# One core, an adaLN transformer block: two thirds of the modulation moved into the first token tile, a bias row behind head 0, a row of maxima in front of the last values

## The chip, the cores and the metric

The kernel runs on one core of one Trainium2 chip. The metric is the device time of one execution in microseconds, as the median of several runs. Its engines are named TensorE (PE, with its weight loads PEld), VectorE (DVE), ScalarE (ACT), GpSimd (POOL) and SyncE (SP), each with its own instruction queue; SP, ACT and POOL also issue DMAs.

## The reference

Input x is 2 x 2048 x 512 in float32. From c (2 x 512) come six vectors for each of the two batches:

```python
mod = (_silu(L0_c) @ L0_wmod).reshape(L0_c.shape[0], 6, 1, -1)
sa, ca, ga, sb, cb, gb = (mod[:, 0], mod[:, 1], mod[:, 2], mod[:, 3], mod[:, 4], mod[:, 5])
ga = (2 * (ga >= 0) - 1) * jnp.maximum(jnp.abs(ga), 0.25)
gb = (2 * (gb >= 0) - 1) * jnp.maximum(jnp.abs(gb), 0.25)
h = _layernorm(x, axis=-1) * (1 + ca) + sa
x = x + ga * attention(h)        # 16 heads of 32, softmax, output projection and bias
h = _layernorm(x, axis=-1) * (1 + cb) + sb
x = x + gb * ffn(h)              # silu(h W1) * (h W3), Hadamard transform of 2048, W2
```

`attention` and `ffn` stand here for the reference's own functions. The first layer norm needs the shift sa and the scale ca alone. The gate ga is first used at the output projection, and sb, cb and gb later still.

## The kernel before

Products that need more than one pass's precision are made from high and low halves: each operand is rounded to fp32r (the high half, written by ScalarE), the difference is the low half (written by VectorE), and three matmuls (high by high, high by low, low by high) are summed. The program is a row of blocks; at the end of each, all engines meet before the next begins.

**Preparation** (`prepare`, lines 57 to 286). SyncE loads the identity, the attention weights in four groups, the first token tile, the modulation's weights `wm` (four chunks of 128 rows by 6 x 512), the output weights `natp`, the Hadamard matrix and the second token tile, through one queue in the order of lines 134 to 146. TensorE transposes the weights (`turn_rows`, L159), ScalarE and VectorE split them. TensorE then transposes the first token tile (`turn_tokens`, L294), makes the modulation's products (`modulate`, L179: per chunk four products of 32 columns into one PSUM bank, SA, CA, SB and CB, each in its own column group, and two, GA and GB, into another bank, in the first two column groups), transposes the output weights (`turn_out`, L172) between them, and at last the modulation (`turn_mod`, L189). ScalarE copies the products out (L236, L237) and writes shifts and scales (L244, L246). VectorE turns the raw gates into gains by four instructions, each waiting for the one before (L281 to L286).

**Projection of queries, keys and values** (`project_qkv`, L369). Eight tiles of 512 tokens. Each tile has NJ = 12 results of 12 matmuls (L538): 8 of queries and keys, 4 of values, in turn in BANKS = 4 PSUM banks. For each tile ScalarE applies shift and scale to the transposed tokens chunk by chunk (`high_parts`, L581), VectorE does the same in full precision for all four chunks (L625) and then makes the four low parts (L630). TensorE waits for all of them (L526, L527) before the tile's first result. ScalarE reads each result (L595, L599) and VectorE makes its low half (L637). Before the results of tile t, ScalarE normalises tile t + 1 (L304) from statistics that VectorE measures (L327 to L339). After result 5 the next tile is transposed. GpSimd makes butterflies of the Hadamard transform on W2 (L704). In the last 15 results TensorE also makes products for head 0's and 1's score maxima (L518), which VectorE reduces (L655); the row of maxima of head 0 is split by L648 and L650. SyncE stores the results in tile order: for each tile the queries and keys (L444) and, after the tile's last result, the values (L446, L447). In front of the first tile it waits for the gains and stores them (L457 to L459). After the last tile's values it sends the two rows of maxima (`send_max_row`, L365), which the first score of head 0 needs (L1027).

**Attention** (`attend`, L780). 32 heads. TensorE goes through 8 pairs of key tiles per head; each has 8 products for the maxima of a later head (L987), alternating with 8 scores (L1036), and then a burst that weighs values (L1047). There are 4 banks for maxima, reduced by VectorE (L1211), and 3 for scores, read by ScalarE's exponential (L1158). GpSimd adds up the exponentials (L1288, L1318), partly by DMAs (L1301); its first sum waits for every stored result (L1339), because its sums lie over their buffers. SyncE first loads the values of heads 0 and 1, queries, keys and values of head 2, the output bias (L963) and the gains. ScalarE's first instruction waits for that bias and copies its high half (L1195, L1196), VectorE's second makes the low half (L1257, L1258). Both are used behind attention only, at L1583.

**Output projection and feed-forward** (`project_and_feed`) follow. Nothing of them is changed.

## Time and profile before

| | us |
|---|---|
| median of 3 runs | 3136.89 |
| lowest and highest run | 3132.02, 3137.76 |
| the profiled execution's own time | 3138.33 |
| its span | 3136.5 |
| TensorE matmuls busy | 3077.2 (98% of the span) |
| VectorE, ScalarE, GpSimd busy | 1878.3, 1516.8, 1418.8 |

The profile covers one execution. In it, times count from the span's start. A group's idle time is that of its engine just before it, with what ended it. TensorE's clock is given as the share of full speed that was granted in a stretch. Matmuls overlap, so one's duration is longer than the step from one to the next. A float32 product of the modulation, whose operands are not split, is two records. The projection's tiles run from about 43 to 375 us, attention from about 379 to 1935, the rest to the end.

### The profile page before, as it was taken

The page shows a single profiled execution, that of the slowest core. Times are in us where ns is not written, and L with a number is a line of the kernel's source. Part 1 is how long each engine was busy: PE and PEld are TensorE (multiplying, and loading weights), DVE is VectorE, ACT ScalarE, POOL GpSimd, SP SyncE. Part 2 cuts the span into 40 slices and gives each one's busy share as a digit, 9 for nine tenths or more (in the row PEclk, how much of TensorE's full clock was granted, in tenths as well). Part 3 has the DMA queues.
Part 4 walks back from the last instruction along what each step waited for, and adds up shares of the span by engine and source line. Part 5 has one row for each costly group of instructions (what it writes and reads, how often), then busy time and mean ns, then how long its engine had stood idle before and what let it go on. Part 6 is the DMA issues. An engine that isn't in the chain of part 4 may idle for free. (4 is left out here: it accounts for less than half of the span.)

```text
span 3136.5 us, 41501 instructions
## 1 busy us (share of the span) xinstructions
PE 3077.2 (98%) x15564; PEld 2103.1 (67%) x15564; DVE 1878.3 (60%) x3184; ACT 1516.8 (48%) x2852; POOL 1418.8 (45%) x489
## 2 busy tenths in 40 slices
PE   6999899999999999999999999999999999999998
PEld 4777655555555555555555554778888888888887
DVE  4444788888888888888888882743332323323232
ACT  3333176666666666666666666543222222222221
POOL 2223088888888888888888885000000000000000
PEclk8999999999999999999999999999999999999999
DMA  6666568888888888888888875762211112111111
GB/s 236 188 193 203 145 128 174 182 181 174 186 182 175 182 181 183 177 182 180 184 180 179 178 162 147 256 217 81 88 44 61 61 48 71 45 60 61 47 57 34
DMA packets 148776, 446.40 MB, mean 142 GB/s; under 512 B 26849, under 2 KB 44513, under 8 KB 113378
## 3 DMA queue, kind: packets, MB, share of 16 engines
q0 software_dynamic: 28592, 204.48, 31.6%
q1 hardware_dynamic: 118930, 239.25, 25.8%
q8 instruction: 127, 2.08, 0.3%
q14 instruction: 71, 0.58, 0.1%
q10 hardware_dynamic: 1056, 0.00, 0.0%
HBM read 166.85 MB, written 80.21 MB: 79 GB/s over the span
## 5 line engine op out<-in xcount | busy, mean ns | idle before, releaser
L1211 DVE TENSOR_REDUCE mxp<-pmax 128x1 f32<-128x512 f32 x1968 | 1202.8, 680 | 245.0 <-PE pmax L987 244.8
L1158 ACT ACTIVATE prob<-pexp 128x512 f32<-128x512 f32 x2023 | 1021.2, 624 | 403.1 <-PE pexp L1036 399.8
L987 PE MATMUL pmax<-k,q 96*128 96x512 f32 x1968 | 813.3, 413 | 4.6 <-PEq L429 4.6
L1036 PE MATMUL pexp<-q,k 98*128 98x512 f32 x2023 | 805.7, 400 | 10.6 <-ACT prob L1158 9.9
L51 PE MATMUL pproj<-h2f,w 128*128 128x512 f32 x3072 | 717.5, 389 | 0.0
L51 PEld LDWEIGHTS pproj<-h2f,w 128*128 128x128 f32 x3072 | 576.5, 188 | 119.7 <-issue 0.3
L1288 POOL TENSOR_TENSOR gsum<-gsum,prob 128x2048 f32<-128x2048 f32 x127 | 583.6, 4595 | 37.3 <-ACT prob L1158 27.8
L987 PEld LDWEIGHTS pmax<-k,q 96*128 96x128 f32 x1968 | 375.0, 191 | 284.1 <-DVE mxp L1211 169.2
L1047 PE MATMUL pctx<-prob,v 128*32 128x512 f32 x4096 | 496.5, 601 | 0.0
L1288 POOL TENSOR_TENSOR gsum<-prob 128x2048 f32<-128x2048 f32 x96 | 458.7, 4778 | 44.3 <-ACT prob L1158 44.2
L1036 PEld LDWEIGHTS pexp<-q,k 98*128 98x128 f32 x2023 | 382.8, 190 | 136.0 <-ACT prob L1158 21.7
L1828 DVE TENSOR_TENSOR hid<-sil,pproj 128x512 f32<-128x512 f32 x128 | 88.1, 688 | 630.4 <-PE pproj L51 628.9
L51 PE MATMUL pturn<-w,gs 128*128 128x512 f32 x1536 | 370.3, 390 | 0.0
L51 PEld LDWEIGHTS pturn<-w,gs 128*128 128x128 f32 x1536 | 287.3, 188 | 59.2
L1710 ACT ACTIVATE sil<-pproj 128x512 f32<-128x512 f32 x128 | 76.7, 599 | 438.6 <-PE pproj L51 438.6
L1047 PEld LDWEIGHTS pctx<-prob,v 128*32 128x32 f32 x4096 | 109.6, 109 | 240.9 <-ACT prob L1158 127.8
L1716 ACT ACTIVATE gs<-hid 128x512 fp32r<-128x512 f32 x128 | 81.1, 634 | 322.5 <-DVE hid L1828 322.5
L1301 POOL DMA_DIRECT2D gsum<-prob x186 | 159.7, 859 | 137.7 <-ACT prob L1158 128.1
L538 PE MATMUL ps_qkv<-ht,wqk 128*128 128x512 f32 x768 | 192.6, 401 | 8.7 <-DVE ht L630 8.7
L538 PEld LDWEIGHTS ps_qkv<-ht,wqk 128*128 128x128 f32 x768 | 145.1, 190 | 45.1 <-issue 10.9
L1318 POOL TENSOR_TENSOR gsum<-gsum 128x2048 f32<-128x2048 f32 x31 | 151.1, 4875 | 0.2 <-DMA gsum<-prob 0.2
L1832 DVE TENSOR_TENSOR gs<-hid,gs 128x512 fp32r<-128x512 f32 x128 | 88.5, 691 | 80.1 <-ACT gs L1716 80.1
(134 smaller groups left out, 1659.6 us busy)
## 6 DMA issues: line engine op xcount, KB each, us to landing
gsum<-prob POOLq DMA_DIRECT2D x187, 1024.0 KB, 7.4
w<-w_scratch SPq DMA_DIRECT2D x128, 256.0 KB, 2.6
q<-q_scratch SPq DMA_DIRECT2D x96, 256.0 KB, 4.4
k<-k_scratch SPq DMA_DIRECT2D x96, 256.0 KB, 6.2
q_scratch<-obq SPq DMA_DIRECT2D x32, 512.0 KB, 5.1
k_scratch<-obq SPq DMA_DIRECT2D x32, 512.0 KB, 3.7
xin<-in_L_attn_query_dram SPq DMA_DIRECT2D x8, 1024.0 KB, 9.3
v_scratch<-vst SPq DMA_DIRECT2D x8, 1024.0 KB, 5.8
```

What stands on the lines that cost most here:

```text
L51: last = pe.matmul(out, stationary(a, c), moving(b, c), start=start and i == 0, stop=stop and i == n - 1)
L538: last = pe.matmul(ps[:, j % BANKS, :], stationary, moving, start=m == 0, stop=m == len(terms) - 1)
L987: pe.matmul(pmax[:, bank, :], qst[slot][0:KR, qt * P:(qt + 1) * P], kst[slot][0:KR, kc * TOK:(kc + 1) * TOK], start=True, stop=True).then_ ...
L1036: pe.matmul(score_bank(g, n), kst[slot_of(g)][:, kt * P:(kt + 1) * P], qst[slot_of(g)][:, j * TOK:(j + 1) * TOK], start=True, stop=True).t ...
L1047: last = pe.matmul(pctx[j * HD:(j + 1) * HD, :], v[:, slot_of(g), kt, :], prob_tile(g, kt)[:, j * TOK:(j + 1) * TOK], start=(kt == 0), sto ...
L1158: act.activation(prob_tile(g, kt)[:, j * TOK:(j + 1) * TOK], score_bank(g, n), ACT.Exp, scale=SCALE).then_inc(exp_done, 1)
L1211: dve.tensor_reduce(mxp[:, par, u // QJ, u % QJ:u % QJ + 1], pmax[:, bank, :], X, ALU.max).then_inc(mx_done, 1)
L1288: pool.tensor_tensor(group_sum(k, g), a, prob_tile(g, kt), ALU.add).then_inc(add_done, 1)
L1301: pool.dma_start(group_sum(k, g), prob_tile(g, kt), accum_op=ALU.add).then_inc(merged[i], 16)
L1318: pool.tensor_tensor(group_sum(1, g), group_sum(1, g), group_sum(UNITS, g), ALU.add).then_inc(add_done, 1)
L1828: dve.tensor_tensor(hid[:, :], sil[:, :], pl[:, h % 2, :], ALU.mult).then_inc(prod, 1)
L1832: dve.tensor_tensor(gs[:, h % 2, LO, :], hid[:, :], gs[:, h % 2, HI, :], ALU.subtract).then_inc(g_lo, 1)
```

## The change

- The modulation's weights are loaded in two parts: the columns of SA and CA (`wm`, NOW = 2 of 6 vectors), in front of them the output weights and behind them the second token tile, and then the other four vectors into a buffer `rest` that is not waited for in the preparation.
- The preparation makes, copies, transposes and applies SA and CA alone, in two column groups of one bank. Two of the four transposes of the output weights come before the token transposes, two behind the modulation's products. The gain instructions leave it.
- In tile 0, behind result 2, TensorE makes the products for GA, GB, SB and CB, one in each column group, in a bank of the token transposes' buffer; ScalarE copies them out behind its read of result 2. Behind result 3 TensorE transposes SB and CB, ScalarE applies them, and VectorE makes the gains. The store of the gains follows tile 0's stores. The transposes of the next tile wait until shift and scale are taken.
- For tile 0, VectorE makes the low part of a chunk right behind its full part, and TensorE waits chunk by chunk in the first result of each tile.
- The store of the last tile's values moves into the attention block, as the first of SyncE's DMAs there, so that the row of maxima is sent before it.
- The bias row's high and low halves are made behind head 0's exponentials and reductions.
- Buffers are laid out anew, with a spare one of 832 floats a partition, and the constants of the modulation live on into the projection.

```diff
@@ prepare, sync @@
-                    sp.dma_start(wm[:, k, :], ins["wmod"][k * P:(k + 1) * P, :]).then_inc(wm_in[k], 16)
+                    sp.dma_start(wm[:, k, :], ins["wmod"][k * P:(k + 1) * P, 0:NOW * D]).then_inc(wm_in[k], 16)
+
+                def load_mod_rest(k):
+                    sp.dma_start(rest[:, k, :], ins["wmod"][k * P:(k + 1) * P, NOW * D:]).then_inc(keep["rest_in"], 16)
...
-                load_mod(0)
-                load_mod(1)
                 sp.dma_start(natp[:, :, :], ins["wproj"].rearrange("(j p) n -> p j n", p=P)).then_inc(natp_in, 16)
-                load_mod(2)
-                load_mod(3)
+                for k in range(DC):
+                    load_mod(k)
+                load_tokens(sp, ins, keep["xin"], 1).then_inc(keep["x_in"][1], 16)
+                for k in range(DC):
+                    load_mod_rest(k)
                 sp.dma_start(had[:, :], ins["hadamard"]).then_inc(keep["had_in"], 16)
-                load_tokens(sp, ins, keep["xin"], 1).then_inc(keep["x_in"][1], 16)
@@ prepare, tensor @@
-                    for i, kinds in enumerate((SHIFTS, (GA, GB))):
-                        for g, x in enumerate(kinds):
-                            last = pe.matmul(ps[g * HD:(g + 1) * HD, i, :], sc[:, k, :],
...
+                    for g, x in enumerate((SA, CA)):
+                        last = pe.matmul(ps[g * HD:(g + 1) * HD, 0, :], sc[:, k, :],
...
+                turn_out(0)
+                turn_out(1)
                 pe.wait_ge(row_hi, QKV * DC)
...
-                modulate(0)
-                modulate(1)
-                for j in range(DC):
-                    turn_out(j)
-                modulate(2)
-                modulate(3)
+                for k in range(DC):
+                    modulate(k)
+                turn_out(2)
+                turn_out(3)
                 turn_mod()
@@ project_qkv, sync @@
+                    if t == TILES - 1:
+                        return
                     sp.wait_ge(out_hi, NJ * (t + 1))
...
-                sp.wait_ge(keep["gains_done"], 1)
...
                     store(t)
+                    if t == 0:
+                        sp.wait_ge(keep["gains_done"], 1)
...
@@ project_qkv, tensor @@
+                def modulate_rest():
+
+                    pe.wait_ge(keep["rest_in"], 16 * DC)
+                    for k in range(DC):
+                        for g, x in enumerate(REST):
+                            at = (WMOD_AT[x] - NOW) * D
+                            last = pe.matmul(pt[g * HD:(g + 1) * HD, 0, :], sc[:, k, :], rest[:, k, at:at + D],
+                                             start=(k == 0), stop=(k == DC - 1))
+                    last.then_inc(rest_mm, 1)
...
-                    if j == 0:
-                        pe.wait_ge(h_hi, DC * (t + 1))
-                        pe.wait_ge(h_lo, DC * (t + 1))
...
+                        if j == 0 and m % len(TERMS) == 0:
+                            pe.wait_ge(h_hi, DC * t + c + 1)
+                            pe.wait_ge(h_lo, DC * t + c + 1)
...
+                        if t == 0 and j == REST_MM:
+                            modulate_rest()
+                        if t == 0 and j == REST_TURN:
+                            turn_rest()
@@ project_qkv, scalar @@
+                        if t == 0 and j == REST_MM:
+                            act.wait_ge(rest_mm, 1)
+                            act.activation(mod[2 * HD:4 * HD, :], pt[2 * HD:4 * HD, 0, :], ACT.Copy).then_inc(rest_read, 1)
+                            act.activation(graw[:, :], pt[0:2 * HD, 0, :], ACT.Copy).then_inc(rest_read, 1)
...
@@ project_qkv, vector @@
+                    for c in range(DC):
+                        whole(c)
+                        if t == 0:
+                            low(c)
...
+                        if t == 0 and j == REST_TURN:
+                            gains()
@@ attend @@
+                store_values(sp, scratch, keep["vst"], v_out, TILES - 1)
                 load_values(0, 0)
...
-                act.wait_ge(bias_in, 16)
-                act.activation(bias[0:1, :], braw[:, :], ACT.Copy).then_inc(bias_hi, 1)
                 for g in range(LAST):
                     step(g)
+                    if g == 0:
+                        act.wait_ge(bias_in, 16)
+                        act.activation(bias[0:1, :], braw[:, :], ACT.Copy).then_inc(bias_hi, 1)
...
-                dve.wait_ge(bias_hi, 1)
-                dve.tensor_tensor(blow[:, :], braw[:, :], bias[0:1, :], ALU.subtract).then_inc(bias_lo, 1)
-                heads(step)
+                for g in range(HEADS):
+                    step(g)
+                    if g == 0:
+                        dve.wait_ge(bias_hi, 1)
+                        dve.tensor_tensor(blow[:, :], braw[:, :], bias[0:1, :], ALU.subtract).then_inc(bias_lo, 1)
```

## Rows read from the trace of the kernel before

**Rows 1.** Stretches, TensorE's: stretch and us, busy (instructions), granted clock, DMA share, GB/s

```profile
6.70:24.70 18.00, 8.37 (x49) 0.93 1.03 405
...
49.20:52.90 3.70, 3.70 (x9) 0.51 0.36 146
60.00:374.10 314.10, 312.39 (x1403) 1.00 0.61 181
...
392.40:397.20 4.80, 4.80 (x11) 0.50 0.00 0
```

**Rows 2.** Timeline of TensorE, 24 to 50 us: start, us, instruction, [idle before <- releaser]

```profile
24.69 3.65 PE L294 MATMUL ps_ht<-ident,xn 128*128 128x128 f32 x16 [7.46 <-ACT xn L304]
28.27 3.95 PE L179 MATMUL ps_prep<-wm,sc 128*32 128x512 f32 x24
32.15 1.09 PE L172 MATMUL ps_prep<-ident,natp 128*128 128x128 f32 x8
...
35.46 3.63 PE L179 MATMUL ps_prep<-wm,sc 128*32 128x512 f32 x24
...
49.18 1.19 PE L538 MATMUL ps_qkv<-ht,wqk 128*128 128x512 f32 x2 [8.73 <-DVE ht L630]
```

**Rows 3.** Timelines of ScalarE, VectorE and GpSimd, 40 to 61 us; last, one line's instructions

```profile
42.85 2.79 ACT L581 ACTIVATE ht<-ps_ht,shift,scale 128x512 fp32r<-128x512 f32 x4 [1.80 <-PEq L123]
...
59.02 1.54 ACT L595 ACTIVATE obq<-ps_qkv 128x512 fp32r<-128x512 f32 x3
...
41.87 0.68 DVE L285 SCALAR_TENSOR_TENSOR gain<-gsign,graw 64x512 f32<-64x512 f32 x1
43.66 2.97 DVE L625 TENSOR_SCALAR full<-ps_ht,scale,shift 128x512 f32<-128x512 f32 x4 [1.11 <-ACT ht L581]
46.54 2.49 DVE L630 TENSOR_TENSOR ht<-full,ht 128x512 fp32r<-128x512 f32 x4
...
51.87 1.80 DVE L335 TENSOR_SCALAR dev<-mv 128x4 f32<-128x4 f32 x1
...
51.26 4.85 POOL L704 TENSOR_TENSOR w2t<-w2n 128x1024 f32<-128x1024 f32 x2 [7.17 <-DMA w2n<-in_L_ffn_W_dram]
...
L335 DVE TENSOR_SCALAR dev<-mv x16: 170/170/1805, 18.4 to 2068.4; 128x4 f32<-128x4 f32 x16
```

**Rows 4.** Timelines of all engines, 370 to 409 us; a DMA to landing; page's L1211

```profile
374.80 0.06 DVE L641 MEMSET mark<- 128x1 f32 x1
...
374.95 3.09 SPq L365 DMA_DIRECT2D q<-mrow  x2
...
378.73 0.77 PE L987 MATMUL pmax<-k,q 96*128 96x512 f32 x1 [4.61 <-PEq L429]
...
392.40 0.80 PE L1036 MATMUL pexp<-q,k 98*128 98x512 f32 x1 [9.31 <-ACT prob L1158]
...
389.81 0.63 ACT L1196 ACTIVATE bias<-braw 1x512 fp32r<-1x512 f32 x1 [15.29 <-DMA braw<-in_L_attn_bproj_dram]
...
391.75 2.08 ACT L1158 ACTIVATE prob<-pexp 128x512 f32<-128x512 f32 x4
...
397.50 4.12 ACT L1158 ACTIVATE prob<-pexp 128x512 f32<-128x512 f32 x8 [0.26 <-PE pexp L1036]
403.41 4.03 ACT L1158 ACTIVATE prob<-pexp 128x512 f32<-128x512 f32 x8 [1.79 <-PE pexp L1036]
...
v_scratch<-vst SPq DMA_DIRECT2D x1, 1024.0 KB, 5.1
...
L1211 DVE TENSOR_REDUCE mxp<-pmax 128x1 f32<-128x512 f32 x1968 | 1202.8, 680 | 245.0 <-PE pmax L987 244.8
```

**Rows 5.** End of head 0, ScalarE and GpSimd; one line's ns: min/median/max

```profile
435.64 1.14 ACT L1158 ACTIVATE prob<-pexp 128x512 f32<-128x512 f32 x2
...
437.69 4.88 POOL L1318 TENSOR_TENSOR gsum<-gsum 128x2048 f32<-128x2048 f32 x1
...
L1238 DVE TENSOR_TENSOR ctxo<-ctxo,recb x31: 681/683/4526, 539.9 to 1927.9; 128x512 f32<-128x512 f32 x31
```

More of the change, by code:

```diff
@@ L34 @@
 SA, CA, SB, CB, GA, GB = range(6)
+NOW = 2
+SPARE = 832
 WMOD_AT = {SA: 0, CA: 1, GA: 2, SB: 3, CB: 4, GB: 5}
@@ L420, in project_qkv @@
         out_lo = sem("a_out_lo")
+        rest_mm = sem("a_rest_mm")
+        rest_read = sem("a_rest_read")
+        rest_turned = sem("a_rest_turned")
+        rest_taken = sem("a_rest_taken")
+        gain_step = sem("a_gain_step")
+        sc, one, mod, graw, gsign, gain, rest = (keep[k] for k in ("sc", "one", "mod", "graw", "gsign", "gain", "rest"))
+        REST = (GA, GB, SB, CB)
+        REST_MM, REST_TURN = 2, 3
         def maxima_of(n):
@@ L462, in _ @@
                     store(t)
+                    if t == 0:
+                        sp.wait_ge(keep["gains_done"], 1)
+                        for i, rows in enumerate((gain[0:B, :], gain[HD:HD + B, :])):
+                            sp.dma_start(scratch["gain"][i], rows).then_inc(gains_out, 16)
                 for i in range(OB):
@@ L622, in low_parts, with whole @@
                     b = t // ST
-                    for c in range(DC):
+                    def whole(c):
                         dve.wait_ge(h_hi, DC * t + c + 1)
@@ L627, in low_parts, with low @@
                                           ALU.add).then_inc(h_full, 1)
-                    for c in range(DC):
+                    def low(c):
                         dve.wait_ge(h_full, DC * t + c + 1)
```

102 lines of the change are left out of this document (60 added, 42 removed).

## The prediction

> **What bounds the kernel now.** I read the busy time by stretch first. From 60 us to the end of the projection of queries, keys and values TensorE is busy for 312.4 of 314.1 us at a granted clock of 1.00 [rows 1], so a tile's work there is a fixed length. What can be won is won where TensorE stands still or at half clock: the preparation, the start of tile 0, and the passage from the projection into attention. For these I went to the timelines of single engines.
>
> In the preparation, the products for the modulation (L179) fill 28.27 to 32.22 and 35.46 to 39.09 us, 7.6 us in all. After them come the copy out of PSUM, the transposes, and on VectorE the gains, which end at 42.55 (41.87 + 0.68); the next block's first ScalarE read is at 42.85 [rows 2, 3]. TensorE next works at 49.18, 8.73 us idle behind VectorE's low halves (L630), and then at half clock (1.2 GHz, full being 2.4): 9 matmuls in 3.7 us against 0.233 us each in the full-clock stretch [rows 1, 2, 3].
>
> At the passage, VectorE ends at 374.86 and ScalarE earlier, but SyncE issues the two rows of maxima from 374.95 to 378.04, and the new block starts at 378.7. TensorE makes 7 products and then sits idle 9.31 us until 392.40: ScalarE's first instruction is the copy of the bias row, which waits 15.29 us for its load and ends at 390.44; a table load of 1.3 us and the first exponential (391.75) stand behind it [rows 4].
>
> A difference of 0.2% (6.3 us) is about what a measurement of this kernel can tell from none.
>
> **1. Preparation.** In L179, four column groups run beside each other. The 12 products of one call (24 records, two passes each) take 3.63 us at full clock [rows 2]. The call's length is that of the groups that carry both a shift or scale and a gate: per chunk four passes one behind the other, so 3.63/8 = 0.45 us a pass or, without the drain at the end, 0.43. The new preparation has two passes per chunk in the busiest group: 8 passes, 3.5 us; the first falls at the end of the half-clock stretch as now, so 3.95 us. It starts at 28.3 as now: two of the four transposes of the output weights go before the token transposes, into the 7.46 us of idle time at 24.69 [rows 2]. They need 2 x 0.55 us, or twice this at half clock; if what they wait for were split only at the gap's end, 1.1 us would be added, no more. Then: products end 32.2; copy 0.6 (32.9); the other two transpose groups 1.1 (33.3); the transposes of the modulation as long as one such group, 0.6 (33.9); ScalarE's two high copies in between, its shift and scale until 34.4; VectorE's last low half, 0.7 behind ScalarE's, until 34.8. The block ends at 34.8 instead of 42.55: **7.8 us earlier**.
>
> Loads: until 24.7 us the queue moves 405 GB/s [rows 1]. What the first products need now (ident, weights, tokens, output weights, a third of the modulation: 7.4 MB) is complete after some 18.5 us of it, near 22 us, under the 28.3 at which it is read; the other 5.3 MB take 13 us more and land near 35, before their use near 49. So zero for these. SyncE's longer list of issues lies beside this too.
>
> **2. Start of tile 0.** VectorE now does four full parts (43.66, 2.97 us) and then four low ones (until 49.03), and TensorE starts at 49.18 with all 12 matmuls of the first result [rows 2, 3]. Chunk by chunk, VectorE's last low part comes later by the lost overlap of dependent pairs, about 4 x 0.1 us, but three chunks, 9 matmuls, are done by then: 9 x 0.233 = 2.1 us. Of the half-clock start, 9 matmuls at 0.42 instead of 0.233, 1.7 us, most falls under VectorE's pace. Bounds: all of it is saved or none; I take 1.1, since the matmuls fed in threes fill much of VectorE's time. Sum: 2.1 + 1.1 - 0.4 = **2.8 us**.
>
> **3. The rest of the modulation in tile 0.** After result 2, 16 products in four equal groups: 8 passes, 3.6 us; later 4 transposes, 0.5 us. TensorE has nothing idle in this tile, so it all counts: **-4.1 us** (upper bound 5.0, two thirds of the 7.6). ScalarE's first read of a result lies 16.2 us after the block's start (59.02 - 42.85) [rows 3]; three reads and the two new copies end near 18.9, while TensorE comes to the new transposes near 20. That is a cover of about 1 us; if it is gone, a wait of up to 1. On VectorE the four gain instructions move from a time at which GpSimd is idle to the butterflies. Beside those, a small instruction (L335) that elsewhere takes 0.17 took 1.80 us, the rest of one butterfly (51.26, two in 4.85) [rows 3]. If each of the four waits for one, they take 10 instead of 2.2 us. Queued behind are the low half of result 4, then SyncE's store. Result 8, 4 banks on, is the first to need it, 4 x 2.8 us later, a turn of the tokens aside: zero, covered by the banks. SyncE's two gain stores stand behind the first tile's stores, where nothing waits. Layout and spare tensors: zero.
>
> Early sum: 7.8 + 2.8 - 4.1 = **6.5 us**.
>
> **4. Row of maxima in front of the last values.** Its issues no longer wait for the last result; they go out under the last tile's matmuls, in which the row is long ready. The block then ends with VectorE at 374.86, and starts again some 0.3 us later, as after the preparation (42.55 to 42.85): 375.2 for 378.7. The store of the last values (5.1 us to land) now stands in front of the values of heads 0 and 1 [rows 4]. Head 0's are wanted by the first weighing, some 9 us in (a table load and 16 exponentials at 0.5); GpSimd's first sum, which may overwrite the buffer being stored, after 8 of them, some 6 us in. Zero, with about 1 us of cover for GpSimd.
>
> **5. Bias row behind head 0.** ScalarE begins with the table load: 375.2 + 1.3 = 376.5 for the first exponential instead of 391.75, **15.25 us** together with part 4. The first eight exponentials took 5.75 us (391.75 to 397.50), TensorE at half clock in 391.75 to 397.2 [rows 1, 4]. TensorE's idle time shrinks to about 1 us twice, so I expect full clock, and VectorE's pace of 0.61 per maximum (1202.8 us for 1968) or ScalarE's of 0.5 (8 in 4.03): 4.0 to 4.9 us [rows 4]. That gives 1.4 (bounds 0, if the clock is low again, and 2.1): **16.7 us**. The copy of the bias (0.63) comes after exponential 63, in ScalarE's idle time of a pair, 1.79 us [rows 4]; the low half (0.68) goes between VectorE's reductions, where 5.8 - 8 x 0.61 = 0.9 is free. Zero, if nothing blocks it.
>
> Total: 6.5 + 16.7 = 23.2 us. The profiled execution took 3138.3 us, its span 3136.5, 1.4 above the median of the runs; off the median 3136.9 that makes **3113.7**.
>
> **Rivals.**
>
> The low half of the bias is blocked (17%). Its two inputs lie in SBUF, and it now runs among GpSimd's sums. The like instruction L1238 mostly took 0.68 us but at worst 4.53 [rows 5]. The merging sum begins at 437.69 and lasts 4.88; the low half would begin 0.65 us behind the last exponential (436.78), at 437.4 [rows 5]. It is ahead by 0.3 us; if the order turns, VectorE stands until 442.6, TensorE fills four banks and waits, 4.4 us: 3118.1. By the Trainium skill (SBUF — State Buffer, Who interferes with whom) a VectorE instruction with two SBUF inputs and a GpSimd one that reads SBUF exclude each other for a whole instruction, and the one that starts first wins; L335 and the longest L1238 agree, and it speaks against this move.
>
> The values arrive late (6%). The first weighing waits where the exponential waited. If head 0's values came as late as the bias row does now, at the queue's end, 389.8 - 378.7 = 11.1 us into the block, TensorE would lose 11.1 - 9.3 = 1.8: 3115.5 [rows 4]. Against: they are second in the queue.
>
> Tile 0 gives the early gain back (5%). If ScalarE came to the two new copies 6.5 us later than worked out, TensorE would wait that long at the new transposes: 3120.2. Against: its preceding work is unchanged.
>
> Slower (2%). TensorE doesn't return to full clock at the start of attention. A pair of eight maxima and eight scores with its weighing takes 4.03 + 1.79 = 5.8 us at full clock [rows 4] and about twice the matmul time, 10.6, at half; each pair costs 4.8. From the fifth pair on the gain of 23.2 is spent, and 7 pairs give 3147.3. Against: it rose within the 4.8 us from 392.40 [rows 1].
>
> **How the numbers follow.** The forecast has 70%. The low end: preparation warm already at the token transposes (1.9 us more), all of the 1.7 saved, 2.1 in part 5, so 26.4 us: 3110.5. The high end: none of the 1.7, a wait of 0.5, 5.0 for part 3, nothing in part 5 beyond 15.25, and the blocked low half: 14.8 us, 3122. The runs of before spread from 3132.0 to 3137.8, so a median may lie a few us lower. Range 3107 to 3122. All but the slower case and its milder half (the clock late by three pairs) are faster by over 0.2%: 0.95 faster, 0.03 the same, 0.02 slower.
>
> **What would show it.** First read of tile 0 near 35.1; first matmul near 37.4, first result done near 42.5; records of the moved products once in tile 0, about 3.6 us long; the block's end near 375 less 6.5; no idle time of TensorE over 1.5 us behind it; the copy of the bias after the 64th exponential; VectorE's low half 0.68 us. It is wrong if TensorE shows a new wait at the new transposes, at result 8, at the first weighing, or after head 0, or if the first pairs run at half clock.

## The result, and the profile after

| | before | changed |
|---|---|---|
| median of the runs, us | 3136.0 (3132.0 to 3137.8) | 3103.8 (3102.0 to 3108.9) |
| profiled execution, us | 3138.3 | 3103.4 |
| its span, us | 3136.5 | 3101.6 |
| mean granted clock of TensorE | 0.992 | 0.996 |

The ratio is 0.9901, 95% interval 0.9885 to 0.9917: 32.2 us less. The forecast was 23.2 us less, 3113.7, with a range from 3107 to 3122; the time lies 3.2 us below the range. The two spans differ by 34.9 us. Marks that both traces have divide them (start of a record; the differences are mine):

| stretch | before | changed | less | forecast |
|---|---|---|---|---|
| start to ScalarE's first read of tile 0 | 42.85 | 33.69 | 9.2 | 7.8 |
| to its first read of tile 1 | 30.1 | 30.8 | -0.7 | -1.3 |
| to the last matmul of the projection | 300.5 | 292.4 | 8.1 | 0 |
| to head 1's first score | 64.5 | 48.5 | 16.0 | 16.7 |
| to the end | 2698.5 | 2696.2 | 2.3 | 0 |

So the three stretches that the change edits came out within 1.4 us of their forecasts, and a stretch of which it edits almost nothing gave 8.1 us.

Start of the changed kernel, TensorE's timeline (start, us, line, operation, idle before and its releaser). It stands against [rows 2]:

```profile
22.25 1.94 PE L173 MATMUL ps_prep<-ident,natp 128*128 128x128 f32 x8 [5.11 <-DVE wv L253]
24.59 2.70 PE L278 MATMUL ps_ht<-ident,xn 128*128 128x128 f32 x16 [0.40 <-ACT xn L288]
27.22 3.63 PE L179 MATMUL ps_prep<-wm,sc 128*32 128x512 f32 x16
...
36.18 4.18 PE L558 MATMUL ps_qkv<-ht,wqk 128*128 128x512 f32 x9 [3.92 <-DVE ht L666]
...
46.85 3.64 PE L481 MATMUL ps_ht<-rest,sc 128*32 128x512 f32 x32
...
53.36 0.46 PE L489 MATMUL ps_ht<-ident,mod 64*128 64x64 f32 x4
```

The preparation's products are one call of 3.63 us, in place of the two that end at 39.09 in [rows 2]. The rest comes in tile 0, 3.64 us and 0.46, and neither row has a wait before it. The first matmul waits 3.92 us for VectorE's low part, where it waited 8.73. The 16 token transposes took 2.70 us: full clock set in among them, earlier than in the profile before. ScalarE's first read of tile 0:

```profile
33.69 2.78 ACT L605 ACTIVATE ht<-ps_ht,shift,scale 128x512 fp32r<-128x512 f32 x4 [0.91 <-PEq L121]
```

On VectorE, two of the four gain instructions before the change, and then all four in the changed kernel, now beside GpSimd's butterflies:

```profile
40.24 0.42 DVE L281 TENSOR_SCALAR gsign<-graw 64x512 f32<-64x512 f32 x1 [3.35 <-ACT graw L237]
...
41.42 0.42 DVE L284 TENSOR_SCALAR graw<-graw 64x512 f32<-64x512 f32 x1
```

```profile
54.71 2.20 DVE L680 TENSOR_SCALAR gsign<-graw 64x512 f32<-64x512 f32 x1
56.94 2.76 DVE L682 SCALAR_TENSOR_TENSOR graw<-gsign,graw 64x512 f32<-64x512 f32 x1
59.74 2.49 DVE L685 TENSOR_SCALAR graw<-graw 64x512 f32<-64x512 f32 x1
62.26 0.68 DVE L687 SCALAR_TENSOR_TENSOR gain<-gsign,graw 64x512 f32<-64x512 f32 x1
```

They took 8.1 us, where the forecast had 2.2 without and 10 with GpSimd beside them, and TensorE shows no wait for it: the four banks covered it. Two of them, L680 and L685, have one SBUF input and were held up too (2.20 and 2.49 us, where they took 0.42).

At the passage, ScalarE, TensorE and SyncE's queue of the changed kernel, against [rows 4]:

```profile
358.59 1.28 ACT L1218 ACT_TABLE_LOAD   x1 [0.64 <-PEq L429]
359.89 2.06 ACT L1218 ACTIVATE prob<-pexp 128x512 f32<-128x512 f32 x4
...
358.63 0.47 PE L1047 MATMUL pmax<-k,q 96*128 96x512 f32 x1 [1.08 <-PEq L429]
...
349.39 1.25 SPq L356 DMA_DIRECT2D q<-mrow  x2
358.59 0.39 SPq L334 DMA_DIRECT2D v_scratch<-vst  x1
```

The row of maxima is issued at 349.39, long before the block's end. The block starts 1.08 us of TensorE's idle time later (4.61 before), ScalarE begins with the table load, and the first exponential starts 1.26 us behind the first product, where 13 us lay between them. TensorE's windows over the same places (length, busy, records, granted clock, DMA share, GB/s), against [rows 1]:

```profile
36.20:39.90 3.70, 3.67 (x8) 0.54 1.04 396
51.50:357.10 305.60, 305.44 (x1405) 1.00 0.62 186
361.10:364.00 2.90, 2.90 (x8) 0.50 1.20 399
```

The tiles run at a clock of 1.00 in both kernels and TensorE hardly waits in either. The 8.1 us of tiles 1 to 7 must therefore lie mostly in shorter steps from matmul to matmul. The values' groups of that stretch, first the kernel before (60 to 374.1 us), then the changed one (51.5 to 357.5):

```profile
L538 PE MATMUL ps_qkv<-wv,ht 128*128 128x512 f32 x384 | 98.0, 396 | 1.5 <-DVE obq L637 1.5
```

```profile
L558 PE MATMUL ps_qkv<-wv,ht 128*128 128x512 f32 x384 | 95.8, 391 | 0.2 <-DVE obq L694 0.2
```

The same 384 matmuls fill 98.0 us in one kernel and 95.8 in the other. From the start of one matmul to that of the next the median is 0.234 us before and 0.227 after in both kinds. The single steps vary, so the sum has to be made from the mean (steps up to 0.26 us): 0.2333 and 0.2274 for queries and keys, 0.2330 and 0.2277 for values. Over the 1008 matmuls of tiles 1 to 7 that is about 6 us. The other 2 us lie in the longer steps (over 0.26 us, the waits), which exceed 0.23 us by 4.9 us in all before and by 2.9 after; the wait of 1.5 us that is gone is most of it. The 6 us were the first thing to explain.

### The profile page after: what moved, and what is told of

The parts are those of the page before. It is cut to its first block and busy times, and to the rows that moved or that the text cites. A ratio compares the mean times of both kernels' runs of the same rounds, so it can differ in the third digit from the quotient of the medians.

```text
span 3101.6 us, 41537 instructions
## 1 busy us (share of the span) xinstructions
PE 3064.5 (99%) x15568; PEld 2100.0 (68%) x15568; DVE 1878.4 (61%) x3184; ACT 1514.1 (49%) x2853; POOL 1418.1 (46%) x489
```

## Experiments 1 to 5: where the shorter step comes from

In tiles 1 to 7 the diff touches nothing but the waits of a tile's first result, now chunk by chunk, and the last tile's store. What it does change there is where the buffers lie. By the order and sizes of the buffers, `ht` (the tokens' high and low halves, one operand of every one of these matmuls) begins at byte 126688 of a partition before, an odd multiple of 32 (96 beyond a multiple of 128), and at 144896 after, a multiple of 512. The weights begin on multiples of 512 in both. The theory was that the start of `ht` sets the step; the rival was that something else in the tile (the table of instructions, other buffers, the DMA traffic) does.

**e1** puts 32 bytes in front of `ht` in the kernel before, which brings it to a multiple of 128 (126720):

```diff
+        sb("pad", [P, 8])
         ht = sb(...)
```

> The kernel before with 32 bytes of padding in front of the normalised tokens' buffer ht and nothing else. In the kernel before ht starts at byte 126688 of its partition (32 past a multiple of 64), here at 126720 (a multiple of 64). Theory A (a matmul whose token operand starts on an odd multiple of 32 bytes is slower): the step from one matmul of the projection to the next falls from 0.234 to 0.227 us in every tile but the last, 1008 x 0.007 = 7 us in all, time near 3129. Theory B (the rest of the change, its order of work or other buffers' places, made the step shorter): the step stays 0.234 and the time is that of before.

Measured: 3128.5 us, ratio 0.9976 (0.9966 to 0.9985), 10 runs. Median step 0.227 us in both kinds. The buffers behind `ht` move with it here; e4 tells the two apart.

**e2** makes the changed kernel's spare longer by 32 bytes, so that `ht` begins 32 beyond a multiple of 128:

```diff
-SPARE = 832
+SPARE = 840
```

> The changed kernel with a spare buffer of 840 instead of 832 floats, so that ht and all buffers behind it start 32 bytes past a multiple of 64. Theory A: the step goes back to 0.234 us, the projection's tiles take 7 to 8 us more, and the gain over before shrinks from 32 to about 24 us (3111). Theory B: the step stays 0.227 and the time is that of the changed kernel (3104).

Measured: 3111.3 us (3110.3 to 3113.5), ratio 0.9921 (0.9905 to 0.9938). Median step 0.234 in both kinds; tile 1's read to the last projection matmul 298.8 us, against 292.4 with the spare of 832.

**e3** sets `SPARE = 16`, with `ht` at 141632, a multiple of 64 and not of 128:

> The changed kernel with a spare buffer of 16 instead of 832 floats: ht starts at 141632, a multiple of 64 but of nothing larger, 3264 bytes lower. Theory A with 64 bytes: step 0.227, time as the changed kernel (3104). Theory A2 (only a larger alignment, 128 to 512 bytes, gives the short step): 0.234, 3111. Theory C (the spare buffer serves to put ht away from something): a step over 0.227.

Measured: 3109.1 us, ratio 0.9911 (0.9894 to 0.9927). Median step 0.229 where `ht` is the moving operand (queries, keys), 0.233 where it is the stationary one (values).

**e4** puts the same 32 bytes behind `ht`, so that the buffers behind it move (results, values, full parts, W2) and `ht` stays. This is the experiment of the rival "other buffers":

```diff
         ht = sb(...)
+        sb("pad", [P, 8])
```

> The kernel before with the 32 bytes behind ht: ht stays on an odd multiple of 32 bytes, the buffers that ScalarE, VectorE and GpSimd write (results, values, full parts, W2) start on multiples of 64. Theory A (it is TensorE's own operand): step 0.234, time as before (3136). Theory D (it is the writes of the other engines that disturb TensorE when they start on an odd multiple): step 0.227, time near 3129, and the first of these kernels would gain by that too.

Measured: 3133.5 us, ratio 0.9992 (0.9982 to 1.0002), 10 runs: 2.6 us less, which isn't clear of noise. Median step 0.234 in both kinds, as before; the 1.5 us wait for `obq` is gone.

**e5** leaves `ht` where the change has it and moves the weights, with the small buffers between them and `ht`, by 32 bytes:

```diff
-SPARE = 832
+SPARE = 824
...
+                    sb(early, "pad_w", [P, 8])
```

> The changed kernel with 32 bytes of padding in front of the attention weights wqk and wv, and the spare buffer 8 floats smaller, so that ht keeps its place at 144896 while both weights start on an odd multiple of 32. Queries and keys then have a shifted stationary operand, values a shifted moving one. Theory A (either operand costs when it is read from an odd multiple of 32): the step is 0.234 us in both kinds of result, time near 3111. Theory E (only the moving operand counts): 0.227 in queries and keys, 0.234 in values, near 3106. Theory F (only the stationary one): the other way round, near 3109. Theory G (only ht itself, by its place against others): 0.227 in both, 3104.

Measured: 3114.8 us in two runs (3118.6 and 3111.0), ratio 0.9931 (0.991 to 0.9953). Median step 0.235 (queries, keys) and 0.234 (values). (The profiled run also has the blocked instruction of experiments 13 and 14, so that the time alone says little here; the step is the reading.)

Equal groups of 24 matmuls each from TensorE's timeline, in this order: before, changed, e1, e2, e3, e4, e5, one kernel a fence:

```profile
109.91 5.84 PE L538 MATMUL ps_qkv<-ht,wqk 128*128 128x512 f32 x24
115.58 8.56 PE L538 MATMUL ps_qkv<-wv,ht 128*128 128x512 f32 x36
```

```profile
100.67 5.70 PE L558 MATMUL ps_qkv<-ht,wqk 128*128 128x512 f32 x24
106.20 8.32 PE L558 MATMUL ps_qkv<-wv,ht 128*128 128x512 f32 x36
```

```profile
109.37 5.70 PE L539 MATMUL ps_qkv<-ht,wqk 128*128 128x512 f32 x24
```

```profile
101.92 5.83 PE L558 MATMUL ps_qkv<-ht,wqk 128*128 128x512 f32 x24
```

```profile
102.62 5.76 PE L558 MATMUL ps_qkv<-ht,wqk 128*128 128x512 f32 x24
108.22 8.56 PE L558 MATMUL ps_qkv<-wv,ht 128*128 128x512 f32 x36
```

```profile
108.99 5.84 PE L539 MATMUL ps_qkv<-ht,wqk 128*128 128x512 f32 x24
```

```profile
102.49 5.85 PE L558 MATMUL ps_qkv<-ht,wqk 128*128 128x512 f32 x24
```

5.84 against 5.70 over 23 steps is 0.006 us a step, 8.56 against 8.32 over 35 is 0.007. For all steps of the stretch (start: bytes past a multiple of 128; the stretch is the table's third, from the first read of tile 1 to the last projection matmul, in us):

| kernel | start of `ht`, of the weights | mean step, ns: queries and keys, values | stretch |
|---|---|---|---|
| before | 96, 0 | 233.3, 233.0 | 300.5 |
| e4 | 96, 0 | 233.3, 233.1 | 298.2 |
| e1 | 0, 0 | 227.4, 227.8 | 292.9 |
| changed | 0, 0 | 227.4, 227.7 | 292.4 |
| changed again (e14) | 0, 0 | 227.4, 227.8 | 293.7 |
| e2 | 32, 0 | 233.0, 233.4 | 298.8 |
| e3 | 64, 0 | 229.4, 233.2 | 298.0 |
| e5 | 0, 32 | 233.4, 233.8 | 298.1 |

The long step goes with the kernel in which an operand starts on an odd multiple of 32 bytes (before, e2, e4, e5), whichever of the two kernels that is; e1 has the short one with nothing of the change but this. The theory holds, and the rivals fall as causes of the step. It is not a property of `ht` either, since it comes with the weights' move too (e5). The size: e1 against e4, which differ by the place of `ht` alone, 5.3 us in the trace and 5.0 in the medians; e2 against the changed kernel's two profiles, 6.4 and 5.1. The other 2 us of the 8.1 aren't the step: e4 has them with `ht` unmoved, and two profiles of the changed kernel differ by 1.3 in the same waits. Where in the chip the 0.006 us arise isn't shown; only starts of 0, 32, 64 and 96 bytes past a multiple of 128 occur here.

## Experiments 6 and 7: the two parts of the passage, one at a time

The forecast has one figure, 15.25 us, for the row of maxima (part 4) and the bias row (part 5) together. The question is what each does alone.

**e6** is the kernel before with the bias behind head 0 only:

```diff
-                act.wait_ge(bias_in, 16)
-                act.activation(bias[0:1, :], braw[:, :], ACT.Copy).then_inc(bias_hi, 1)
...
+                    if g == 0:
+                        act.wait_ge(bias_in, 16)
+                        act.activation(bias[0:1, :], braw[:, :], ACT.Copy).then_inc(bias_hi, 1)
```

(and VectorE's low half likewise).

> The kernel before with the bias row's two halves made behind head 0 and nothing else. The forecast's working: the first exponential no longer waits for the bias load but for the row of maxima, which lands near 380.1 us, so it starts near 381 instead of 391.75, 10.9 us, and the first pair at full clock gives another 1.4: 12.3 us faster, 3124. A rival, that the values' load or the queue behind it takes the wait's place: under 9 us faster.

Measured: 3132.8 us, ratio 0.9988 (0.9978 to 0.9998). Last projection matmul to head 1's first score 53.4 us, 11.1 less than before; but head 1 itself lasts 55.3 us instead of 48.4, since the low half was blocked. So the median gained 3.5 us where 12.3 were expected. An execution with the low half free would have come near 3125 (an estimate: 3136.4 less 11.1), and none of the ten runs is under 3130.3. VectorE and GpSimd, then TensorE, in e6:

```profile
425.08 5.83 DVE L1262 TENSOR_TENSOR blow<-braw,bias 1x512 fp32r<-1x512 f32 x1
...
425.53 4.83 POOL L1321 TENSOR_TENSOR gsum<-gsum 128x2048 f32<-128x2048 f32 x1
...
431.57 0.79 PE L987 MATMUL pmax<-k,q 96*128 96x512 f32 x1 [3.87 <-DVE mxp L1212]
```

**e7** is the kernel before with the row of maxima in front of the last values only (its `send` moved as in the change, `store_values` behind it in the next block):

> The kernel before with the row of maxima in front of the last values' store, which goes to the start of attention, and nothing else. The block ends 3.5 us sooner. Theory H (the parts need each other): the bias row, for which the first exponential still waits, stands behind one more megabyte in the queue, some 3.6 us, so its landing stays near 389.8 us and the time stays that of before within 1 us. Rival (the parts add up): 3.5 us faster, 3132.5.

Measured: 3136.7 us, ratio 1.0001 (0.9991 to 1.001). The block starts 3.5 us sooner, and all of it is given back: TensorE, ScalarE and the queue in e7:

```profile
374.03 0.47 PE L997 MATMUL pmax<-k,q 96*128 96x512 f32 x1 [1.08 <-PEq L436]
...
391.57 0.79 PE L1046 MATMUL pexp<-q,k 98*128 98x512 f32 x1 [15.65 <-ACT prob L1168]
...
388.98 0.63 ACT L1206 ACTIVATE bias<-braw 1x512 fp32r<-1x512 f32 x1 [15.63 <-DMA braw<-in_L_attn_bproj_dram]
...
373.99 0.39 SPq L372 DMA_DIRECT2D v_scratch<-vst  x1
```

The bias row's load stands behind the store of the last values and the heads' loads in the same queue, so ScalarE's copy starts 16.7 us behind the last projection matmul (388.98, the matmul 372.3), where it was 16.3 before (389.81 in [rows 4], 373.5). Alone the parts give 0 and 11.1 us at this passage, together 16.0. The row of maxima is worth its 5 us only when nothing late stands behind it.

## Experiments 13 and 14: the blocked low half

**e14** is the changed kernel again, as it is:

> The changed kernel as it is, beside the next one. Theory: its executions fall into two groups, near 3103 where the low half takes 0.68 us and near 3109 to 3112 where it takes 5.8.

Measured: 3110.9, 3103.8, 3111.8 and 3103.7 us, median 3107.4, ratio 0.9905 (0.9888 to 0.9921). The four runs form two groups 7.6 us apart. The four of the result section show the same, less evenly: three from 3102.0 to 3104.2, one at 3108.9; that the low half was blocked in that one isn't shown, since it has no profile. The profile fell in the upper group here and in the lower there. VectorE and GpSimd at the start of head 1, first the changed kernel's first profile, then e14:

```profile
404.61 0.68 DVE L1322 TENSOR_TENSOR blow<-braw,bias 1x512 fp32r<-1x512 f32 x1
...
404.46 0.85 POOL L1364 DMA_DIRECT2D gsum<-prob  x1 [1.62 <-ACT prob L1218]
405.06 4.88 POOL L1381 TENSOR_TENSOR gsum<-gsum 128x2048 f32<-128x2048 f32 x1
```

```profile
405.44 5.83 DVE L1322 TENSOR_TENSOR blow<-braw,bias 1x512 fp32r<-1x512 f32 x1
...
405.29 0.85 POOL L1364 DMA_DIRECT2D gsum<-prob  x1 [1.59 <-ACT prob L1218]
405.89 4.82 POOL L1381 TENSOR_TENSOR gsum<-gsum 128x2048 f32<-128x2048 f32 x1
...
411.93 0.80 PE L1047 MATMUL pmax<-k,q 96*128 96x512 f32 x1 [3.87 <-DVE mxp L1272]
```

And a window of TensorE in e14 behind it (columns as above):

```profile
412.00:418.00 6.00, 6.00 (x24) 0.60 0.85 175
```

The order of the two starts is the same, VectorE's record 0.45 us ahead of GpSimd's sum in both. In one execution it takes 0.68 us, in the other it ends with the sum, 5.83 us. In the second TensorE fills its banks and idles 3.87 us, from 408.1 to 411.93. The granted clock falls to half at 410.0, within this idle time, and stays there until 416.8 (the window's 0.60), so TensorE works 4.9 us at half clock. From head 1's first score to head 2's it is 54.7 us instead of 48.5: 6.3 us, which is the idle time and half of the 4.9. Over the seven profiles in which the low half was held up, head 1 took 54.2 (e10) to 55.7 us (e5), so 5.8 to 7.3 more. Of the rest of the two profiles' difference of 7.5 us, 0.8 lies ahead of head 1.

**e13** moves the low half behind the first reduction of head 1, that is, surely into the sum:

```diff
+                        if g == 1 and n == 1:
+                            dve.wait_ge(bias_hi, 1)
+                            dve.tensor_tensor(blow[:, :], braw[:, :], bias[0:1, :], ALU.subtract).then_inc(bias_lo, 1)
...
-                    if g == 0:
-                        dve.wait_ge(bias_hi, 1)
-                        dve.tensor_tensor(blow[:, :], braw[:, :], bias[0:1, :], ALU.subtract).then_inc(bias_lo, 1)
```

> The changed kernel with the low half of the bias row one reduction later, behind the first maximum of head 1 instead of in front of it, about 1.5 us on, when GpSimd's merging sum has begun. Theory K (it is blocked by a running GpSimd sum): it takes 3.5 to 4.5 us in every execution, TensorE idles 2 to 4 us in head 1, and the median is 4 to 6 us over the undisturbed runs of the changed kernel, 3107 to 3109, with no low runs. Rival (the 5.8 us belong to something at the boundary of the heads): 0.68 us, 3103.

Measured: 3111.9 us (3111.7 to 3112.2), ratio 0.9922 (0.9906 to 0.9939): one group, the upper one. In e13:

```profile
406.56 4.21 DVE L1305 TENSOR_TENSOR blow<-braw,bias 1x512 fp32r<-1x512 f32 x1
...
405.39 4.84 POOL L1381 TENSOR_TENSOR gsum<-gsum 128x2048 f32<-128x2048 f32 x1
...
411.44 0.79 PE L1047 MATMUL pmax<-k,q 96*128 96x512 f32 x1 [3.41 <-DVE mxp L1272]
```

Its start is behind the sum's, and all four runs are in the upper group; head 1 lasts 55.0 us. By the Trainium skill (SBUF — State Buffer, Who interferes with whom) the two exclude each other for a whole instruction. Every row here agrees: each blocked record ends 0.5 to 0.6 us behind GpSimd's sum. For which of the two wins, a start 0.45 us ahead in the record doesn't decide: it won in the changed kernel's first profile alone and lost in six (e5, e6, e8, e9, e10, e14). In the two other profiles with a free low half at this place GpSimd waited a little for its data first, and the lead was 0.75 us (e3) and 1.09 (e2): there the 0.68 us were over before the sum began. The trace doesn't show when an instruction first asks for its operands.

## Experiments 8 and 9: preparation and start of tile 0

**e8** puts the two groups of output-weight transposes back behind the products. The theory was that they, in the idle time ahead of the token transposes, brought the clock's rise forward:

```diff
-                turn_out(0)
-                turn_out(1)
...
+                turn_out(0)
+                turn_out(1)
```

> The changed kernel with the first two groups of output weight transposes behind the modulation's products instead of before the token transposes. In the changed kernel TensorE's clock rose at 26.8 us, in the kernel before at 29.0. Theory I (these transposes keep TensorE at work and so bring the clock up one step sooner): the token transposes take 3.6 instead of 2.7 us again, the first read of tile 0 comes at 35.5 to 36.5 instead of 33.7 us, time 2 to 3 us over the changed kernel's (3106). Rival (the clock rose by chance of its phase): the clock rises at 26.8 all the same and the block ends within 1 us of before, 34.2 at most.

Measured: 3114.3 us (3106.6 to 3116.1), ratio 0.9923 (0.9905 to 0.994). ScalarE's first read of tile 0 is at 36.0 us, against 33.4 to 34.9 in the eleven profiles of kernels that keep the change's order there. TensorE's start in e8:

```profile
23.85 3.65 PE L278 MATMUL ps_ht<-ident,xn 128*128 128x128 f32 x16 [5.97 <-ACT xn L288]
27.43 3.63 PE L179 MATMUL ps_prep<-wm,sc 128*32 128x512 f32 x16
...
33.15 1.23 PE L173 MATMUL ps_prep<-ident,natp 128*128 128x128 f32 x8 [1.07 <-DVE wp L258]
```

By itself e8 gives the numbers that the theory named: 36.0 us, and 3.65 for the token transposes. But without the early transposes the clock is full from 27.4 us, and with them from anywhere between 25.6 (e10) and 28.7 us (e3); the changed kernel itself had 26.2 in one profile and 27.7 in the other, with 3.65 us for the token transposes. So the theory isn't borne out: an early rise goes with the execution, not with the order. Of the 1.4 us that the early gain has over its forecast in the first profile, 1.0 is left in the second (34.09). What the order does bring is 1.2 to 2.6 us, of which the transposes' own time is 1.1. Some of e8's total is again a blocked low half (5.82 us in its profile).

**e9** lets tile 0 wait for all four chunks, as before:

```diff
-                        if j == 0 and m % len(TERMS) == 0:
-                            pe.wait_ge(h_hi, DC * t + c + 1)
-                            pe.wait_ge(h_lo, DC * t + c + 1)
+                        if j == 0 and m == 0:
+                            pe.wait_ge(h_hi, DC * (t + 1))
+                            pe.wait_ge(h_lo, DC * (t + 1))
```

(and the four low parts after the four full ones).

> The changed kernel with the start of tile 0 as before: VectorE makes four full parts and then four low ones, TensorE waits for all. The forecast's working: TensorE's first matmul of tile 0 comes at about 6.3 us behind the first full part (40.3) instead of 36.2, and the first result is done 2.8 us later (1.7 to 3.4 by the clock's phase): 3106.5 against the changed kernel's 3103.8. Rival (tile 0 is bound by ScalarE, whose first read lies 16 us behind the block's start): no difference, 3104.

Measured: 3115.8 us (3112.9 to 3117.6), ratio 0.9935 (0.992 to 0.995). First read of tile 0 to first read of tile 1: 34.5 us, against 30.8 in the changed kernel's first profile and 31.0 in its second. So part 2 is worth 3.5 to 3.7 us there, above the forecast's 2.8. The total holds a blocked low half too (5.83 us in the profile). TensorE in e9 waits 7.76 us for the first matmul, where it was 8.73 before and 3.92 in the changed kernel:

```profile
41.19 10.55 PE L558 MATMUL ps_qkv<-ht,wqk 128*128 128x512 f32 x36 [7.76 <-DVE ht L666]
```

## Experiments 10, 11, 12 and 15: a better version

Two edits that the findings suggest. **e10** makes the rest of the modulation ahead of tile 0's first result, where TensorE waits for VectorE anyway, in the fourth of the projection's banks:

```diff
-                            last = pe.matmul(pt[g * HD:(g + 1) * HD, 0, :], sc[:, k, :], rest[:, k, at:at + D],
+                            last = pe.matmul(ps[g * HD:(g + 1) * HD, 3, :], sc[:, k, :], rest[:, k, at:at + D],
...
-                        if t == 0 and j == REST_MM:
+                        if t == 0 and j == 0:
```

(and ScalarE's four copies ahead of its reads of the results).

> The changed kernel with the rest of the modulation made ahead of tile 0, in the 3.9 us in which TensorE waits for VectorE's first low part, into the fourth result bank; its transposes stand behind result 0, its reads by ScalarE in front of the second tile's normalisation. Theory (the moved products cost 3.6 us of a full TensorE where they are): they start when their weights land, near 35 us, and end near 38.6, 1 us after TensorE would have begun and before VectorE's last low part (40.4), so 3 to 3.6 us are saved: 3100.5. Rival (the weights land later than 35 us, or the start is bound by VectorE and then ScalarE): under 1.5 us saved.

Measured: 3110.8, 3101.7, 3112.2, 3111.4 and 3103.3 us, ratio 0.9908 (0.9895 to 0.9922): two groups again. The rows of TensorE in e10:

```profile
36.51 5.00 PE L481 MATMUL ps_qkv<-rest,sc 128*32 128x512 f32 x32 [4.51 <-DMA rest<-in_L_wmod_dram]
41.44 3.01 PE L558 MATMUL ps_qkv<-ht,wqk 128*128 128x512 f32 x12
```

The weights `rest` land near 36 us, and the products wait for them. The forecast put that landing near 35. In place of the 4.1 us of part 3 little is won: head 1's first score is at 404.8 instead of 405.4 us, and tile 0 takes 30.3 us instead of 30.8. What the late landing leaves is taken by the clock, which is at half from 35.9 to 39.3 us. The same products in e12 and in e15, which have this edit too, one kernel a fence:

```profile
35.17 3.64 PE L490 MATMUL ps_qkv<-rest,sc 128*32 128x512 f32 x32 [2.72 <-DMA rest<-in_L_wmod_dram]
```

```profile
35.45 6.27 PE L490 MATMUL ps_qkv<-rest,sc 128*32 128x512 f32 x32 [3.12 <-DMA rest<-in_L_wmod_dram]
```

In e12 the clock stays full from 26.4 us through the whole projection, and tile 0 takes 27.9 us; in e15 it is at half from 34.0 to 40.8, and tile 0 takes 30.2. So the expected 3 us are there in one profile of three.

**e11** takes the bias out of attention altogether. Its row is loaded in the projection's third tile into a free row of the gates' buffer and split there, where VectorE and GpSimd's sums don't meet:

```diff
+                        if t == 2 and j == 1:
+                            dve.wait_ge(bias_hi, 1)
+                            dve.tensor_tensor(gsign[0:1, :].bitcast(F32R), graw[0:1, :], keep["bias"][0:1, :],
+                                              ALU.subtract).then_inc(bias_lo, 1)
...
-                    if g == 0:
-                        dve.wait_ge(bias_hi, 1)
-                        dve.tensor_tensor(blow[:, :], braw[:, :], bias[0:1, :], ALU.subtract).then_inc(bias_lo, 1)
```

(and likewise the load, ScalarE's high half and the store of the low one).

> The changed kernel with the bias row loaded and split in the projection's third tile instead of behind head 0, so that no VectorE instruction with two SBUF inputs stands beside GpSimd's merging sum. Theory J (in some executions that low half takes 5.8 us, TensorE idles 3.9 and then runs at half clock): the runs lie together near 3102 and none is over 3106, the median 1 to 4 us under the changed kernel's. Rival (the high runs come from the clock's phase at the start alone): the spread of the changed kernel, 3102 to 3109, stays.

Measured: 3106.5 us (3105.5 to 3108.6), ratio 0.9909 (0.9893 to 0.9924). One group of runs; head 1 takes 48.4 us. TensorE has two waits of 0.7 us in the tiles (for a copy of values and for a part of W2) that the changed kernel's first profile lacks; its second has the like (0.7 and 0.5).

**e12** has both edits, and **e15** is e12 again beside e14:

> The two edits together: the rest of the modulation ahead of tile 0, and the bias row in the projection's third tile. If both theories hold, 3 to 3.6 us plus 1 to 4 us under the changed kernel: near 3099. If the edits take from one another, no better than the better one alone.

> The version with the rest of the modulation ahead of tile 0 and the bias row in the projection's third tile, as it is. Theory: one group of runs, 3102 to 3106, its median 0 to 4 us under the changed kernel's beside it, and its slowest run under the changed kernel's slowest. Rival: no difference.

Measured: e12 3104.7 us (3103.5 to 3108.2), ratio 0.9904 (0.9889 to 0.9919); e15 3105.0 (3104.2 to 3105.9), ratio 0.9901 (0.9885 to 0.9918). Beside e15 the changed kernel had 3107.4. The intervals of the two ratios overlap almost wholly, so no faster median is shown. What the runs show is that the upper group is gone: the slowest of these eight runs took 3108.2 us, the changed kernel's slowest 3111.8. The changed kernel's lower group (3102.0 to 3104.2) still lies a little below e15's runs; why isn't shown.

## Why the prediction was right or wrong, point by point

**Layout and spare tensors: zero.** This is the step of part 3 that failed, and it put the time outside the range. The diff says "buffers are laid out anew", and the step priced that at nothing without asking where each operand of the largest group of matmuls would begin. It was worth 5 to 6 us of the 9.9 by which the median lies below the forecast: 5.0 (e1 against e4, medians) to 6.4 (e2 against the changed kernel, in the tiles). With it undone, e2's median of 3111.3 lies inside the range. Of e1's whole 7.6 us (3136.1 to 3128.5) e4 has 2.6 with `ht` in its old place. Of the rest of the 9.9, 0.9 is the median of before, which was 3136.9 in the forecast and 3136.0 beside the changed kernel; in the profiles 2 us of waits in tiles 1 to 7, 1.4 of the preparation and the 2.3 of the last stretch lie on the same side. The trace of before had a hint: from start to start its projection matmuls stood at 0.233 us, the prediction's own figure, and the feed-forward's products of the same shape, whose operands begin on multiples of 128, at 0.227. "A tile's work there is a fixed length" took the clock and the busy share for the whole story.

**1, preparation, 7.8.** Measured 9.2. The order of events came as written: products of 3.63 us in one call, transposes in the idle time, the block's end 9 us sooner. The step said that the products start "at 28.3 as now"; they started at 27.22, since the token transposes ran partly at full clock. The profiles beside e8 show this in some executions and not in others of the same order. The low end of the range had named it ("warm already at the token transposes"), and in the second profile (e14) it was absent and the gain 8.8.

**2 and 3, start of tile 0 and the moved products, 2.8 and -4.1.** Together -0.7 measured for -1.3. In tile 0, e9 gives part 2 as 3.5 to 3.7, and with part 3 alone (e9 against before, 34.5 and 30.1) the stretch is 4.4 longer. Both are somewhat larger than forecast and of opposite sign. The moved products took 3.64 and 0.46, as stated. No wait appeared at the new transposes. The gain instructions took 8.1 us of the "10 instead of 2.2", and cost TensorE nothing. These steps held.

**4 and 5, the passage, 16.7.** Measured 16.0. The first exponential, at 359.89, comes 3.0 us behind the start of the last projection matmul. The 1.4 us for the clock came only in part: the window 361.1 to 364.0 still has 0.50, and the ninth exponential started 5.1 us behind the first, where it was 5.75 before and the forecast had 4.0 to 4.9. Part 4's "375.2 for 378.7" came true as a start of the block, and is worth nothing alone (e7: 0; e6, part 5 alone: 11.1). The 15.25 held because it was worked out for both together.

**The blocked low half, 17% and 4.4 us.** The mechanism was right and both numbers were too small. By their times it occurs in two of e14's four executions, in one of the result section's four, and in all ten of e6, and it costs 6.3 us in e14, because the step counted TensorE's idle time (3.87 measured) but not the half clock that reaches beyond it. The result section's runs mostly drew the free side. Had the upper group been the median, the time would have been near 3111, inside the range by luck, with the layout's gain hidden in it. The step's support was in part loose: L335 has one SBUF input and isn't a case of the rule on two that the step cites, though it was held up like the gain instructions above.

**The other rivals.** The first weighing started at 368.1, 9.2 us behind the first score (358.9), with no wait for the values. Tile 0 gave nothing back. The start of attention returned to full clock at 364.1, so the forecast's case "slower" didn't come.

**The rest, 2.3 us.** In the last head the profile before has three half-clock stretches of 3.4 us (from 1882.4, 1889.2 and 1940.4), the changed kernel's first profile one (from 1906.9). This isn't a gain of the change: the same stretch, from head 1's first score to the end, took 2695.6 us in e1, which is the kernel before but for 32 bytes, and 2698.3 in e12, which has the whole change. What sets these stretches stays open.

## What to carry to other kernels

When a change adds, drops or resizes a buffer, write down the start address of each operand of the largest group of matmuls, before and after. If the step from matmul to matmul differs between two stretches of the same shape at the same clock, look at these addresses before the code, and take the price from the mean step, not from the median. A small VectorE instruction with two SBUF inputs doesn't belong near the start of a long GpSimd one, however free VectorE looks; price it as a wait of the whole sum, with TensorE's way back to full clock on top. Where two parts shorten one passage, work out a price for both together, as was done here, and test each alone before only one of them is carried over.

## What the runs showed of the hardware that was not expected

- A 128x512 matmul in fp32r steps by 0.227 us when both operands begin on multiples of 128 bytes of a partition, and by 0.234 to 0.235 (medians; the means are 0.227 to 0.228 and 0.233 to 0.234) when either begins on an odd multiple of 32 bytes (before, e2, e4: the tokens; e5: the weights). On a multiple of 64 alone it was 0.229 with that operand moving and 0.233 with it stationary (e3).
- Whether VectorE or GpSimd goes first isn't set by the order of their records: a lead of 0.44 or 0.45 us gave 0.68 us in one profile and 5.82 or 5.83 in six.
- VectorE instructions with one SBUF input can be held up beside GpSimd's too: TENSOR_SCALAR of 64x512 took 2.20 and 2.49 us there, and 0.42 before.
- An idle time of TensorE of 3.9 us in the middle of attention goes with 6.8 us at half clock, 410.0 to 416.8 in e14, of which TensorE works 4.9.
- At the start, the granted clock rises at 25.6 to 30.1 us, in different profiles of nearly the same work (e10, e1).
